# Layer 3 attention with the row sums in the value columns, inverted 32 columns wide

## The reference

```python
def _L3_xattn_ref(q, k, v, gamma):
    N_HEAD = 8
    B, Dq, Lq = q.shape            # 64, 64, 256
    Dv, Lk = (v.shape[-2], v.shape[-1])
    h = N_HEAD
    dq = Dq // h                   # 8
    dv = Dv // h                   # 8
    qh = q.reshape(B, h, dq, Lq)
    kh = k.reshape(B, h, dq, Lk)
    vh = v.reshape(B, h, dv, Lk)
    scale = 1.0 / jnp.sqrt(jnp.asarray(dq, dtype=q.dtype))
    qk = jnp.einsum('bhdq,bhdl->bhql', qh, kh) * scale
    sm = jax.nn.softmax(qk, axis=-1)
    ret = jnp.einsum('bhql,bhdl->bhdq', sm, vh)
    ret = ret.reshape(B, Dv, Lq)
    return gamma * ret
x = x + _L3_xattn_ref(_layernorm(x, axis=-1), ctx_2048, ctx_2048, L3_xattn_gamma)
```

## Time and profile before

| | |
|---|---|
| median of 3 runs | 2297.29 us (2294.67 to 2300.11) |
| the profiled execution's own time | 2271.76 us |
| its span, first to last instruction | 2269.8 us |
| busy: PE, DVE, ACT, POOL | 1875.2, 1606.8, 993.9, 1008.8 us |
| mean granted TensorE clock | 0.925 |
| DMA: data moved, mean rate | 173.16 MB, 76 GB/s |

### The profile page before, as it was taken

One profiled execution on the slowest core, in us unless ns is written; L12 is line 12 of the kernel. 1 busy time (PEld: TensorE's weight loads), 2 busy tenths in 40 slices (PEclk: granted clock), 3 DMA queues, 4 the chain that ended last, 5 costly groups with the idle time before them and its releaser, 6 DMA issues. The chain is left out here.

```text
span 2269.8 us, 46910 instructions
## 1 busy us (share of the span) xinstructions
PE 1875.2 (83%) x16123; PEld 1402.6 (62%) x16126; DVE 1606.8 (71%) x3825; ACT 993.9 (44%) x2454; POOL 1008.8 (44%) x1267
## 2 busy tenths in 40 slices
PE   6989745498875988888987897788888887989993
PEld 5879522387664777777776786444444443557772
DVE  7965722469667888899886665888888885553446
ACT  3732221134233544555543332366666665533330
POOL 3410026524364666666665200355555654563331
PEclk9989856699997999999998999799999999999996
DMA  7821046600150000000003110155445550533337
GB/s 218 290 76 52 10 125 171 198 6 12 57 144 11 1 0 0 0 0 0 0 0 57 29 29 1 33 101 106 101 97 99 101 105 7 157 107 97 107 108 238
DMA packets 137374, 173.16 MB, mean 76 GB/s; under 512 B 30961, under 2 KB 115105, under 8 KB 137185
## 3 DMA queue, kind: packets, MB, share of 16 engines
q1 hardware_dynamic: 127377, 148.54, 25.2%
q0 software_dynamic: 9808, 22.23, 3.3%
HBM read 113.40 MB, written 56.20 MB: 75 GB/s over the span
## 5 line engine op out<-in xcount | busy, mean ns | idle before, releaser
L2854 DVE TENSOR_REDUCE mx<-bank 128x2 f32<-128x512 f32 x512 | 322.7, 677 | 82.3 <-PE bank L2724 80.5
L2826 ACT ACTIVATE e<-bank 128x512 f32<-128x512 f32 x512 | 282.1, 597 | 177.2 <-PE bank L2746 177.2
L2677 POOL TENSOR_TENSOR es<-e 128x256 f32<-128x256 f32 x256 | 183.8, 734 | 149.2 <-ACT e L2826 146.4
L1914 POOL TENSOR_TENSOR q_l<-q_l,rot_l 64x512 f32<-64x512 f32 x128 | 162.3, 1268 | 129.6 <-DVE rot_l L2112 129.6
L2759 PE MATMUL bank<-e,val 128*32 128x256 f32 x2048 | 137.9, 386 | 36.8 <-ACT nd L2821 36.7
L2746 PEld LDWEIGHTS bank<-q,k 64*128 64x128 f32 x1024 | 78.0, 186 | 120.8 <-ACT e L2826 79.2
L2746 PE MATMUL bank<-q,k 64*128 64x256 f32 x1024 | 129.9, 331 | 18.8 <-ACT e L2826 14.1
L1946 PE MATMUL bank<-qcT,wq_abs 96*128 96x128 f32 x1024 | 126.0, 283 | 0.0
L2724 PE MATMUL bank<-k,q 62*128 62x256 f32 x1024 | 112.9, 299 | 15.6 <-DVE mx L2854 11.2
L3038 POOL DMA_INDIRECT y<-y,y_row x71 | 68.7, 968 | 126.9 <-DVE y L3313 123.9
L1946 PEld LDWEIGHTS bank<-qcT,wq_abs 96*128 96x128 f32 x1024 | 120.2, 196 | 2.5
(11 more groups left out here) (450 smaller groups left out, 4961.0 us busy)
## 6 DMA issues: line engine op xcount, KB each, us to landing
k<-k_parts SPq DMA_DIRECT2D x128, 128.0 KB, 4.2
q<-q_parts SPq DMA_DIRECT2D x128, 128.0 KB, 3.4
got<-rows SPq DMA_DIRECT2D x71, 129.0 KB, 2.2
k_parts<-k_parts_a SPq DMA_DIRECT2D x64, 128.0 KB, 3.0
moe_rows<-zero_a SPq DMA_DIRECT2D x16, 512.0 KB
w<-in_e0w SPq DMA_DIRECT2D x16, 512.0 KB, 3.7
q_parts<-parts SPq DMA_DIRECT2D x64, 128.0 KB, 2.4
parts_y<-y SPq DMA_DIRECT2D x32, 256.0 KB, 4.7
```

Source lines behind the costliest of these rows:

```text
L1914: nc.gpsimd.tensor_tensor(q[64:P, j, four(m), :], q[64:P, j, four(m), :], rot[64:P, j, four(m), :], ALU.add).then_inc(s["rope_added"], 1)
L2677: nc.gpsimd.tensor_tensor(es[:, n, :], e[:, n, 0, :], e[:, n, 1, :], ALU.add).then_inc(s["sum_ready"], 1)
L2826: nc.scalar.activation(e[:, slot(i, r), :, :].rearrange("p k n -> p (k n)"), scoresT(r)[:, :], ACT.Exp).then_inc(s["exp_ready"], 1)
L2854: v.tensor_reduce(mx[:, a.n, r % 2, 0, at:at + 2], scores(r)[:, :].rearrange("p (a n) -> p a n", a=2), AX.X, ALU.max, negate=True).then_in ...
```

## The change

The row sums no longer have matmuls of their own. Each head's 8 value columns stand in a block of 32 columns of `val`, of which 24 are zero; one of these is now 1.0 (`sums = DQ3 * (i ^ 1)`), so the readout gives the head's sum in one row. Even quads go to the left half of the bank and odd quads to the right, since the sum's row of one parity is a value row of the other. `gam` is multiplied into the values. The 16 x 256 sums of a tile are then carried by DMAs: `gather` into `den` (128 partitions x 32), VectorE inverts 32 columns, `store_inverse` writes them to the DRAM tensor `rec_rows`, and `load_inverse` reads each row back onto 8 partitions of `rec`. GpSimd multiplies 128x512, adds the halves and adds to x, three tiles later than the readout. `nd` has 4 buffers. The zero rows of `rec_rows` are written once, in the stage before.

Each batch of a tile now has its own half of the partitions (`batch_rows`), where before each half had four heads of either batch. `q` and `k` are loaded by four DMAs of 256 KiB a tile in place of eight of 128 KiB. The readout of a quad is split over the two half-steps.

```diff
+            sp.wait_ge(s["p_ones"], 5)
+            sp.dma_start(c.rec_rows.rearrange("n a r l -> (n a r) l"), c.rec3[0:64, 0, 0, :]).then_inc(s["p_loaded"], 16)
...
+                        sums = DQ3 * (i ^ 1)
+                        nc.gpsimd.memset(c.val3[:, :, :, i, :, sums:sums + 1], 1.0).then_inc(s["p_ones"], 1)
...
-def head_rows(ap, both, g):
-    return ap[:, :, 2 * H3 * both:2 * H3 * both + 2 * H3, :].rearrange("a c (b g h) l -> g (a c) b (h l)", b=2, g=2)[g]
-def copied_rows(ap, both, g, b):
-    return head_rows(ap, both, g)[:, b, :].unsqueeze(1).broadcast_to([2 * DQ3, 2, H3 // 2 * D])
+def batch_rows(ap, t, b):
+    heads = (2 * t + b) * H3
+    return ap[:, :, bass.ds(heads, H3), :].rearrange("a c h l -> (a c) (h l)")
...
             def load(a):
...
-                for g, base in enumerate(BASE3):
-                    for b in range(2):
-                        sp.dma_start(whole(q[base:base + R, 2 * a.n + b, :]),
-                                     copied_rows(c.q_parts, a.t, g, b)).then_inc(s[qk_loaded[a.n]], 16)
-                    for m in range(2):
-                        sp.dma_start(whole(k[base + 2 * DQ3 * m:base + 2 * DQ3 * (m + 1), both, :]),
-                                     head_rows(c.k_parts, a.t, g)).then_inc(s[qk_loaded[a.n]], 16)
+                for b, base in enumerate(BASE3):
+                    q_rows, k_rows = batch_rows(c.q_parts, a.t, b).unsqueeze(1), batch_rows(c.k_parts, a.t, b).unsqueeze(0)
+                    sp.dma_start(whole(q[base:base + R, a.n, :]),
+                                 q_rows.broadcast_to([2 * DQ3, 2, H3 * D])).then_inc(s[qk_loaded[a.n]], 16)
+                    sp.dma_start(whole(k[base:base + R, a.n, :]),
+                                 k_rows.broadcast_to([2, 2 * DQ3, H3 * D])).then_inc(s[qk_loaded[a.n]], 16)
...
+            def gather(a):
+                b = a.n % 2
+                sp.wait_ge(s["out_copied"], tile_ready(a.t))
+                sp.wait_ge(s["inv_ready"], tile_ready(a.t) - 2)
+                for h in range(2):
+                    sp.dma_start(den[64 * h:64 * h + 64, b, :], nd[DQ3 * (1 - h)::2 * DQ3, a.n, h, :]).then_inc(s[den_loaded[b]], 16)
+            def store_inverse(a):
+                b = a.n % 2
+                sp.wait_ge(s["inv_ready"], tile_ready(a.t))
+                if a.exists(-2):
+                    sp.wait_ge(s[rec_loaded[b]], 32 * uses(a))
+                for h in range(2):
+                    sp.dma_start(c.rec_rows[b, h, h::2, :], inv[64 * h:64 * h + 64, b, :]).then_inc(s[rec_stored[b]], 16)
+            def load_inverse(a):
+                b = a.n % 2
+                sp.wait_ge(s[rec_stored[b]], 32 * (uses(a) + 1))
+                sp.wait_ge(s["on_ready"], tile_ready(a.t) - 2)
+                for h in range(2):
+                    sp.dma_start(rec[:, b, h, :], c.rec_rows[b, h, :, :].unsqueeze(1).broadcast_to(
+                        [2 * H3, DQ3, D])).then_inc(s[rec_loaded[b]], 16)
...
             def tile(a):
+                if a.exists(-2):
+                    store_inverse(a.to(-2))
                 if a.exists(1):
                     lay_rows(a.to(1))
                 if a.exists(AHEAD):
                     store(a.to(AHEAD))
+                if a.exists(-2):
+                    load_inverse(a.to(-2))
+                if a.exists(-1):
+                    gather(a.to(-1))
                 if a.exists(BUF):
                     sp.wait_ge(s["turned_ready"], unit_ready(a.t, 3, 3))
...
-                nc.gpsimd.tensor_tensor(on[:, :], nd[:, a.n % 2, 0, :], rec[:, :], ALU.mult).then_inc(s["on_ready"], 1)
+                nc.gpsimd.tensor_tensor(on[:, :, :], nd[:, a.n, :, :], rec[:, b, :, :], ALU.mult).then_inc(s["on_ready"], 1)
+                nc.gpsimd.tensor_tensor(on[:, 0, :], on[:, 0, :], on[:, 1, :], ALU.add).then_inc(s["on_added"], 1)
...
+            def read(a, i, lt):
+                side = slice(i % 2 * D, i % 2 * D + D)
+                for r in range(4):
+                    g = group(r)
+                    last = nc.tensor.matmul(readout[32 * g:32 * g + 32, side], val[:, a.n % 2, g, i, lt, :],
+                                            e[:, slot(i, r), lt, :], start=(i == 0 and lt == 0),
+                                            stop=(i >= 2 and lt == DK - 1), skip_group_check=True)
...
-                        if (i, r) == (1, 0) and a.exists(-1):
+                        if (i, r) == (0, 3) and a.exists(-1):
                             out_copy(a.to(-1))
-                        if (i, r) == (2, 3) and a.exists(AHEAD):
+                        if (i, r) == (1, 2) and a.exists(AHEAD):
                             high(a.to(AHEAD))
...
-                v.reciprocal(rec[:, :], nd[:, a.n % 2, 1, :]).then_inc(s["rec_ready"], 1)
+                dve.wait_ge(s[den_loaded[b]], 32 * (uses(a) + 1))
+                v.reciprocal(inv[:, b, :], den[:, b, :]).then_inc(s["inv_ready"], 1)
```

More of the change, by code:

```diff
@@ L2232, in _ @@
             for n in range(BUF3):
-                both = slice(2 * n, 2 * n + 2)
-                for g, base in enumerate(BASE3):
-                    k_rows = head_rows(c.k_parts, n, g)
-                    for m in range(2):
-                        rows = slice(base + 2 * DQ3 * m, base + 2 * DQ3 * (m + 1))
-                        sp.dma_start(whole(c.k3[rows, both, :]), k_rows).then_inc(s["p_loaded"], 16)
+                for b, base in enumerate(BASE3):
+                    k_rows = batch_rows(c.k_parts, n, b).unsqueeze(0)
+                    sp.dma_start(whole(c.k3[base:base + ROWS3, n, :]),
+                                 k_rows.broadcast_to([2, 2 * DQ3, H3 * D])).then_inc(s["p_loaded"], 16)
                 sp.dma_start(c.vt3[:, n, :, :], c.d["ctx_cols"][n]).then_inc(s["p_loaded"], 16)
             for n in range(BUF3):
-                both, cols = slice(2 * n, 2 * n + 2), slice(2 * n * H3, 2 * n * H3 + 2 * H3)
+                cols = slice(2 * n * H3, 2 * n * H3 + 2 * H3)
                 sp.wait_ge(s["p_low"], n + 1)
@@ L2554, in place, with group @@
         def place(t, i, r):
-            return BASE3[r % 2], 2 * (t % BUF) + r // 2, i * D
+            return BASE3[r % 2], t % BUF, (QU * (r // 2) + i) * D
+        def group(r):
+            return 2 * (r % 2) + r // 2
         class At:
@@ L2634, in _ @@
             run(sp, tile)
+            end = At(NT // BUF - 1, BUF - 1)
+            store_inverse(end.to(-1))
+            gather(end)
+            load_inverse(end.to(-1))
+            store_inverse(end)
+            load_inverse(end)
         @block.gpsimd
@@ L2670, in split_max @@
                                         ALU.subtract).then_inc(s["max_split"], 1)
[L2672 to L2677, removed]
             def x_low(a):
@@ L2712, in _ @@
             run(pool, tile)
-            finish(At(NT // BUF - 1, BUF - 1))
+            for n in (3, 2, 1):
+                finish(At(NT // BUF - 1, BUF - n))
         @block.tensor
@@ L2778, in tile @@
                         turn_max(a.to(1), unit_ready(a.t, 1, 2))
-                    for p, part in enumerate((read, read_lengths)):
+                    for p in range(2):
                         if turning and p == 1:
@@ L2785, in tile @@
                         if i > 0:
-                            part(a, i - 1)
+                            read(a, i - 1, p)
                         elif a.exists(-1):
-                            part(a.to(-1), QU - 1)
+                            read(a.to(-1), QU - 1, p)
             for n in range(LEAD):
@@ L2798, in _ @@
             run(pe, tile)
-            read(At(NT // BUF - 1, BUF - 1), QU - 1)
-            read_lengths(At(NT // BUF - 1, BUF - 1), QU - 1)
+            for p in range(2):
+                read(At(NT // BUF - 1, BUF - 1), QU - 1, p)
         @block.scalar
@@ L2891, in _ @@
             end = At(NT // BUF - 1, BUF - 1)
-            dve.wait_ge(s["rec_ready"], tile_ready(end.t) - 1)
+            dve.wait_ge(s["inv_ready"], tile_ready(end.t) - 2)
             finish_stats(nc, c, sch, EARLY)
-            invert(end)
-            stats(end.to(-1))
-            stats(end)
+            for n in (2, 1):
+                invert(At(NT // BUF - 1, BUF - n))
+            for n in (3, 2, 1):
+                stats(At(NT // BUF - 1, BUF - n))
 def stage_l3_moe(nc, c):
```

118 lines of the change are left out of this document (55 added, 63 removed).

## The result

| | before | changed kernel |
|---|---|---|
| time, median of 4 runs each | 2295.98 us (2290.09 to 2300.11) | 2401.22 us (2396.10 to 2406.51) |
| ratio, 95% interval | | 1.046 (1.042 to 1.050) |
| predicted | | 2382 us (2290 to 2480) |
| profiled execution, span | 2271.76, 2269.8 us | 2406.51, 2404.7 us |

What follows compares the result with a forecast made beforehand. The k load on two DMA engines was to bound the attention stage at 18.1 us a tile; +76.5 us in the stage and +8.5 at its end, +85 on the median of 2297.3, gave 2382 us (2290 to 2480).

Steps and rivals of the forecast that it cites:

- The k transfer on two engines: Attention stage's k load: a source with a zero-stride outermost extent of 2 runs on two of 16 DMA engines; chance 0.70.
- Rival 1: k transfer: the destination's 32 rows alone decide, giving 16 engines and a hidden load; 2210 us, chance 0.14.
- The burst: A tile's q, k and vt load: 303 KB on each of the two engines at 22 GB/s, 13.8 us.
- The 22 GB/s: Rate taken for each of the two DMA engines, from q<-rows moving alone at 44 GB/s; bounds 8.7 and 23 GB/s.
- The period: SyncE's loop per tile: 1.3 start, 13.8 burst, 0.6 receipt, four issues of 0.6, 18.1 us.
- the receipt: In SyncE's loop, the time after the burst until the store of the inverses counts as landed: 0.6 us.
- The stage and the end: Attention stage to its last readout +76.5 us; from there to the last statistics, with nothing hiding the round trip, +8.5.
- The compute part: Attention tile without DMA limits: half-steps of 1.24 us, quads of 2.9, reciprocal 0.28, 11.9 us a tile.
- Rival 2: k load on two engines, but above 23 GB/s each or with receipt and issues overlapped: 2285 to 2310 us, chance 0.08.
- Rival 3: k load on two engines at 8.7 to 15 GB/s, period 24 to 39 us: 2540 to 2950 us, chance 0.06.
- Rival 4: Load spread over engines, but VectorE's reciprocal waits for the gathered sums, 13.2 us a tile: 2248 us, chance 0.02.
- The 25.5 us: Whole kernel: runs' median 2297.3 us above the profiled execution's 2271.8, reason not in the trace; carried into the forecast.

Runs made afterwards that it cites:

- e1: The changed kernel with each 256 KiB k transfer cut into two of 128 KiB, 16 rows outermost at the source, no zero-stride broadcast: 2220.5 us, ratio 0.964 to before.
- e2: The kernel before with its four 128 KiB k transfers each filling 32 rows from a source of 2 zero-stride copies, nothing else changed: 2379.11 us, ratio 1.034 to before.
- e8: The changed kernel with k loaded by 16-row transfers as in e1 and the inverses loaded one tile later: 2215.15 us, ratio 0.963 to before.
- e3: The changed kernel with batch 0's k still by the zero-stride broadcast, batch 1's in two transfers of 16 rows: 2312.3 us, ratio 1.006 to before.
- e1 again: The same kernel as e1, timed again as reference for the second group of runs: 2222.53 us, ratio 0.966 to before.
- e5: The changed kernel with SyncE's load of the inverses moved behind the q/k/vt load: 2556.97 us, ratio 1.110 to before.
- e6: e1 with the next tile's rows laid on SyncE ahead of the store of the inverses: 2248.66 us, ratio 0.977 to before.

## Why the prediction was right

**The k transfer on two engines: right.** It carried the forecast, and e1 and e2 show it from both sides. Rival 1 (the destination alone decides) falls with them, and with the share of 0.13. Its figure, 2210 us, is what e1 came within 11 us of: it priced the rest of the change nearly rightly (11.9 us a tile, where e1 has 12.5), and put the transfer wrong.

**The burst: 13.8 us predicted, 13.2 measured** (1712.0 to 1725.2). 303 KB in 13.2 us are 23.0 GB/s on each of the two engines. But this is a mean of two rates. With k alone the two move 55 GB/s, 27.5 each, which is above the 23 that I had taken as the upper bound of the rate; early in the burst, with q on all sixteen, they must be slower. The 22 GB/s came from transfers of 512-byte pieces that had the engines to themselves; that it also fits the mean of a burst of 8 KB pieces, fast alone and slow beside others, is luck. The Trainium skill, DMA: Bandwidth & Descriptors (Specifications), puts an engine at about 27 GiB/s, which is 29 GB/s. The trace comes near it while such a transfer is alone (27.5 GB/s); as a price for the whole burst that figure is too fast here: an estimate by it is 10.5 us, where 13.2 were measured.

**The period: 18.1 predicted, 18.75 to 18.9 measured.** The step that was mis-sized is what follows the burst. I gave 0.6 us to the receipt. From the last k bytes to SyncE's next issue it is 1.4 (1725.2 to 1726.58), and the share stays at 0.15 until 1726.5. The store of the inverses has to move there behind the k bytes, which I had counted in the engines' total but not in this sum; how much of the 1.4 is its bytes and how much its receipt, no row splits. The four issues from the load of the inverses to the burst took 2.9 us (1726.58 to 1729.50), not 4 x 0.6. Start 1.2 + 13.2 + 1.4 + 2.9 = 18.7 against 1.3 + 13.8 + 0.6 + 2.4. From the first to the last burst (1466.0 and 1975.7) there are 27 periods of 18.88 us, so this term was short by 27 x 0.78 = 21 us.

**The stage and the end.** +96.0 measured against +76.5, the 19.5 by the period; the end +7.9 against +8.5. The median difference was 105 where the forecast had 85. One slip in the sum has no weight: the 35.4 us for three tiles are 3 x 11.8, and its own 11.9 makes 35.7.

**The compute part: right, and hidden.** 1.24 us a half-step at full clock (with ScalarE's wait 2.92 us a quad, 1715.26 to 1718.18, where the prediction had 2.9) and a reciprocal of 343 ns (predicted 280) stand in the rows above. The tile of 11.9 us cannot be read from the changed kernel; e8, where DMA holds it least, has 12.0. In the changed kernel the clock was not full. At a tile's start, after the gap, its granted clock was down to half, 1.2 GHz, and two half-steps took 2.16 and 1.97 us (1707.71 to 1709.87 to 1711.84). That lies beside the burst: TensorE is done with the tile at 1720.7 and then waits 6.3 us for its rows, so the slow half-steps cost nothing by themselves in this tile.

**Rival 2** (two engines, but quicker, or with receipt and issues overlapped) had one thing right: the rate alone passes 23 GB/s. The overlap did not come. **Rival 3** falls with the 13.2 us. **Rival 4**, VectorE waiting for gathered sums, was looked for and is 16.9 us over the whole stage, 7.98 of them at the end.

Left open: why the two engines were slower in e3's burst than its sum had them. The 25.5 us that the prediction added for the quick profiled execution of before have a place in the record, though no cause. From the last statistics to the end before took 343.1 us (1926.73 to 2269.8), with the same code e2 took 364.1, e1 again 364.3 and the changed kernel 361.8. So some 20 us of it lie in the feed-forward step behind this stage, and taking the difference over into the forecast was right.

## What to carry to other kernels

Read the outermost extent on both sides of every DMA, the source too: a view that repeats rows by a zero stride outermost moved 512 KiB a tile on two engines of sixteen, at a cost of 181 us in the whole stage, while the same bytes as four transfers of 16 rows were all but hidden (0.9 us a tile). A narrow transfer harms more than its own reader: what stands behind it on the same engines (rows, stores, their receipts) lands late too, and when the queue that issues the next burst waits for one of those, the two form a loop whose period is the sum of both. In an in-order queue the place of a step decides what its bytes stand behind; ask of each move who reads it next (e5 cost 156 us more, e6 26).

## What the hardware showed that I had not expected

- Two engines with pieces of 8 KB moved 27.5 GB/s each when they were alone; sixteen together had 23 each at best in the earlier trace rows, and 18 (287/16) at the start of the burst shown above. Over bursts shared with the q transfers the two had 23.0 (changed kernel) and about 20 (e3).
- GpSimd's product of 128x128 values with one number a row took 603 ns, where the copy in its place had taken 287 (L2659 in the trace of before, the mean of 64). It was hidden here.
- TensorE's granted clock over 300 us of the stage was 0.81 in the changed kernel, and 1.00 in e1. With 5.6 us of idling a tile it fell to the lower of its two levels (0.50, 1.2 GHz), and the first work after the gap took up to 1.7 times as long (2.16 against 1.24 us). In e2, where TensorE waited 2.3 us a tile for its rows, it was 0.95.
